# Copying attention values by DMA instead of ScalarE, stacking query and key parts with fewer transfers, and a new order table

## The reference

```
xn = layernorm(x)
s  = attention0(xn)      # 16 heads of 8, full 512x512 softmax      -> streams "A" and "head"
g  = silu(ffn0(xn))      # one of 8 experts per token               -> done for all rows before the loop
x  = x + s * g
xn = layernorm(x)
s  = attention1(xn)      # 16 local-window heads + 8 latent heads   -> stream "B"
g  = silu(ffn1(xn))      # two layers, each as below                -> stream "F" (and "finish")
x  = x + s * g

ffn1, per layer: h = shift_token(x); q, k, v = split(h @ wqkv)      # 8 heads of 64
                 q, k = rotary(l2norm(q) * qs), rotary(l2norm(k) * ks)
                 o = softmax(8 * q k^T, window of 64 and the one before) v ;  x = x + o @ wo
                 h = layernorm(shift_token(x)) ; x = x + (a * gelu(g)) @ w2, with a, g = split(h @ w1 + b1)
```

## Time and profile before

| | |
|---|---|
| median of 3 executions | 4537.1 us (4527.5 to 4545.72) |
| the profiled execution | 4527.5 us, its span 4525.7 us |
| busy PE | 3647.1 us (81%) |
| busy DVE | 2793.2 us (62%) |
| busy ACT | 2096.0 us (46%) |
| busy POOL | 734.8 us (16%) |
| DMA | 141.05 MB, 8.8% of 16 engines for the hardware queue |
| mean granted TensorE clock | 0.895 |
| the 13 full iterations | 813.3 to 4074.4 us of the span: 250.9 us each |

### The profile page before, as it was taken

How to read it: one execution, slowest core, us unless ns; L and a number is a source line. 1 busy time by engine, 2 the same in 40 slices (tenths; PEclk the granted TensorE clock), 3 DMA queues, 4 the chain that set the end, 5 groups by cost and what they waited for, 6 DMA issues and landing times. The chain is left out here.

```text
span 4525.7 us, 98207 instructions
## 1 busy us (share of the span) xinstructions
PE 3647.1 (81%) x41689; PEld 2067.7 (46%) x41816; DVE 2793.2 (62%) x5577; ACT 2096.0 (46%) x3692; POOL 734.8 (16%) x383
## 2 busy tenths in 40 slices
PE   3486788888878788888888788888888787888866
PEld 3372335444454545354444545353444445453543
DVE  5114467666666767666666666676666666676644
ACT  1122345555545454545545454545555454545533
POOL 3410011111111111111111111111111111111111
PEclk9996689898999999898989999898999998998978
DMA  4351101010000101010100101010100001010000
GB/s 144 117 170 45 26 21 26 23 26 19 20 18 23 25 21 27 24 26 24 26 19 11 27 22 26 21 26 24 26 19 26 13 23 25 21 27 23 4 10 3
DMA packets 130874, 141.05 MB, mean 31 GB/s; under 512 B 18005, under 2 KB 112703, under 8 KB 129855
## 3 DMA queue, kind: packets, MB, share of 16 engines
q1 hardware_dynamic: 120656, 105.16, 8.8%
q0 software_dynamic: 9712, 28.85, 2.1%
HBM read 81.27 MB, written 35.39 MB: 26 GB/s over the span
## 5 line engine op out<-in xcount | busy, mean ns | idle before, releaser
L964 ACT ACTIVATE prob_a<-bank 128x512 f32<-128x512 f32 x1024 | 585.5, 599 | 541.8 <-PE bank L909 538.3
L1016 DVE TENSOR_REDUCE nmax_a<-bank 128x1 f32<-128x512 f32 x768 | 513.1, 688 | 393.9 <-PE bank L882 388.4
L1358 POOL TENSOR_TENSOR rn<-ss,minus_half 128x16 f32<-128x16 f32 x128 | 489.8, 3827 | 1264.5 <-DVE ss L1632 1264.5
L1517 ACT ACTIVATE area<-bank 128x512 f32<-128x512 f32 x640 | 349.5, 601 | 291.0 <-PE bank L1409 223.5
L909 PE MATMUL bank<-Qst_a,Kst_a 74*128 74x512 bf16 x1024 | 411.5, 422 | 68.8 <-DVE nmax_a L1016 62.9
L896 PE MATMUL bank<-prob_a,V_a 128*9 128x512 f32 x2048 | 320.5, 703 | 51.1 <-ACT prob_a L964 48.3
L882 PE MATMUL bank<-Kst_a,Qst_a 72*128 72x512 bf16 x768 | 330.9, 431 | 31.3 <-ACT prob_a L964 15.9
L1635 DVE TENSOR_TENSOR prob_f<-area,rotf 128x1024 f32<-128x1024 f32 x256 | 308.0, 1225 | 1.0
L1409 PE MATMUL bank<-wqkv_s,hT 128*128 128x512 f32 x384 | 215.5, 685 | 82.9 <-issue 71.7
L1005 DVE TENSOR_REDUCE nmax_a<-bank 128x1 f32<-128x512 f32 x256 | 169.5, 687 | 109.7 <-PE bank L870 107.0
L909 PEld LDWEIGHTS bank<-Qst_a,Kst_a 74*128 74x128 bf16 x1024 | 98.2, 100 | 297.3 <-DVE nmax_a L1016 190.7
(11 more groups left out here) (282 smaller groups left out, 7153.0 us busy)
## 6 DMA issues: line engine op xcount, KB each, us to landing
Qst_a<-dq_a SPq DMA_DIRECT2D x192, 96.0 KB
Kst_a<-dk_a SPq DMA_DIRECT2D x192, 96.0 KB
dq_a<-prob_a SPq DMA_DIRECT2D x80, 128.0 KB, 2.4
dk_a<-prob_a SPq DMA_DIRECT2D x48, 128.0 KB, 2.4
area<-xs_d SPq DMA_DIRECT2D x39, 128.0 KB, 4.5
ys_d<-otok_f SPq DMA_DIRECT2D x39, 128.0 KB, 1.8
xs_d<-prob_f SPq DMA_DIRECT2D x4, 1024.0 KB, 8.9
x_a<-in_x_in SPq DMA_DIRECT2D x16, 256.0 KB, 2.9
```

The source lines that it names most:

```text
L964: nc.scalar.activation(dst, bk.full(act, product)[0:rows, :], func, **kw).then_inc(a_emptied["act"], 1)
L1016: nc.vector.tensor_reduce(out=nmax_a[:, g, t, j:j + 1], in_=bk.full(dve, f)[:], op=ALU.max, axis=AX.X, negate=True).then_inc(emptied, 1)
L1358: nc.gpsimd.tensor_tensor(rn[:, t % 2], ss[:, t % 2], minus_half[:], ALU.pow).then_inc(f_root, 1)
L1517: ins = nc.scalar.activation(dst, fk.full(act, product)[rows, cols], func, **kw)
```

## The change

Three edits and a new table.

**Values.** ACT writes only `V_f`. At the slot `QKV + 13` of each layer SP waits until the last V_f tile is brought, and copies `V_f` into `V_s` with two transfers: 64 partitions x 2080 floats, and 64 partitions x 1560 floats. PE waits for both (`f_moved`) before the first `values_f` of a layer. The initial memset of V_s's ones column goes, since the copies carry the column.

**Stacks.** `spill` still issues 8 transfers, but writes three full rotations of the q parts and three copies of the k parts (6 x 384 KB in place of 8 x 128 KB). `load_stack` then needs 2 transfers of 72 partitions for a group in place of 6 of 24 partitions. An inner row in DRAM is up to 3 KB, not 1 KB.

**Tables.** A_TIMES, H_TIMES and the three tables of F_AT for PE, ACT and DVE hold other numbers.

```diff
-A_TIMES = ((14, 15, 106, 113), (0.5, 2.7, 101.3, 102.4))
+A_TIMES = ((14, 15, 106, 113), (3.2, 3.7, 102.3, 103.4))
...
-        dq_a, dk_a = scratch("dq_a", [H0, 2 * SPLIT - 1, D0, T]), scratch("dk_a", [H0, SPLIT, D0, T])
+        dq_a, dk_a = scratch("dq_a", [H0, SPLIT, D0, SPLIT, T]), scratch("dk_a", [H0, SPLIT, D0, SPLIT, T])
...
-            for c in range(2 * SPLIT - 1):
-                sp.dma_start(dq[:, c], parts_q[:, c % SPLIT, :]).then_inc(s, 16)
-                if c < SPLIT:
-                    sp.dma_start(dk[:, c], parts_k[:, c, :]).then_inc(s, 16)
+            for i in range(SPLIT):
+                sp.dma_start(dq[:, i, :, 0:SPLIT - i, :], parts_q[:, i:SPLIT, :]).then_inc(s, 16)
+                if i:
+                    sp.dma_start(dq[:, i, :, SPLIT - i:SPLIT, :], parts_q[:, 0:i, :]).then_inc(s, 16)
+                sp.dma_start(dk[:, i], parts_k).then_inc(s, 16)
...
-            for i in range(SPLIT):
-                sp.dma_start(Qst[rows * i:rows * i + rows], q_rows[D0 * i:D0 * i + rows]).then_inc(s, 16)
-                sp.dma_start(Kst[rows * i:rows * i + rows], k_rows).then_inc(s, 16)
+            for stack, d in ((Qst, dq), (Kst, dk)):
+                sp.dma_start(stack[0:STACK], d[h:h + n].rearrange("h i d c t -> (i d c) h t")).then_inc(s, 16)
...
+            for l in range(DEPTH):
+                yield LAYER_AT + LAYER * l + QKV + 13
+                sp.wait_ge(*fk.brought(("fv", l, NT - 1), "act"))
+                sp.dma_start(V_s[0:FW], V_f[0:FW]).then_inc(f_moved, 16)
+                sp.dma_start(V_s[FW:P, 1:NT], V_f[FW:P, 0:NT - 1]).then_inc(f_moved, 16)
...
+                    if c == 0:
+                        pe.wait_ge(f_moved, 32 * (l + 1))
...
-                        nc.scalar.activation(V_s[0:FW, t, :, 0:FD], v[0:FW], ACT.Copy)
-                        yield at + 0.9
-                        if t + 1 < NT:
-                            nc.scalar.activation(V_s[FW:P, t + 1, :, 0:FD], v[FW:P], ACT.Copy)
-                            yield at + 1
```

More of the change, by code:

```diff
@@ L58 @@
 A_GROUP = (15, 37, 60, 84)
-A_TIMES = ((14, 15, 106, 113), (0.5, 2.7, 101.3, 102.4))
+A_TIMES = ((14, 15, 106, 113), (3.2, 3.7, 102.3, 103.4))
 B_TIMES = ((0, 1, 4, 5, 17, 25), (121.6, 126, 135.3, 142, 166, 185))
-H_TIMES = ((0, 30), (122.1, 194.3))
+H_TIMES = ((0, 30), (122.1, 195.9))
 FEED = ((0, 180), (0, 296))
 F_AT = {"sync": FEED, "gpsimd": FEED,
-        "tensor": ((1, 4.3, 4.6, 6.42, 8.55, 10.2, 11, 11.5, 11.8, 12.1, 13, 20.1, 21, 27.2, 29, 35.2, 37, 40, 42,
[7 rows of a table removed]
-        "scalar": ((1, 6.17, 8.55, 11.2, 12.3, 12.4, 20.4, 27, 27.2, 40, 42.6, 47, 60.8, 65.2, 68.5, 88.5, 90.2, 90.6,
[4 rows of a table removed]
-        "vector": ((4, 6.55, 7.1, 8.8, 12.5, 14, 22, 25.2, 26, 28.5, 29, 30, 34, 38.2, 39, 77, 79, 83, 87, 95, 101,
[4 rows of a table removed]
+        "tensor": ((1, 4.6, 6.05, 8.05, 8.55, 11.2, 11.5, 13, 19.8, 20.1, 21, 37, 46.4, 48.4, 50.8, 52, 53.1, 53.4,
[6 rows of a table added]
+        "scalar": ((1, 6.17, 8.55, 11.2, 12.3, 20.1, 20.3, 27.2, 40, 42.6, 52, 56.4, 65.2, 68.5, 78, 90.4, 90.6, 93.2,
[3 rows of a table added]
+        "vector": ((4, 6, 6.55, 7.1, 8.3, 8.8, 13.4, 13.6, 20, 20.5, 22, 28.5, 30, 33, 38.2, 39, 52.8, 53.1, 57.5, 79,
[6 rows of a table added]
 B_AT = 5
@@ L680, in _ @@
                         outputs_out(j - 2)
-                for V in (V_f, V_s):
-                    nc.vector.memset(V[:, :, :, FD:FD + 1], 1.0)
+                nc.vector.memset(V_f[:, :, :, FD:FD + 1], 1.0)
         def engine_sems(p):
@@ L705, in mixer_kernel @@
         a_var, a_rstd, b_var, b_rstd = sem("a_var"), sem("a_rstd"), sem("b_var"), sem("b_rstd")
-        f_sq, f_root, f_rot, f_mparts = (sem(n) for n in ("f_sq", "f_root", "f_rot", "f_mparts"))
+        f_moved, f_sq, f_root, f_rot, f_mparts = (sem(n) for n in ("f_moved", "f_sq", "f_root", "f_rot", "f_mparts"))
         f_wo, f_mid = sem("f_wo"), sem("f_mid")
@@ L796, in spill @@
         def spill(sp, parts_q, parts_k, dq, dk, s):
-            for c in range(2 * SPLIT - 1):
-                sp.dma_start(dq[:, c], parts_q[:, c % SPLIT, :]).then_inc(s, 16)
-                if c < SPLIT:
-                    sp.dma_start(dk[:, c], parts_k[:, c, :]).then_inc(s, 16)
-        SPILLED, STACKED = (3 * SPLIT - 1) * 16, 2 * SPLIT * 16
-        def load_stack(sp, dq, dk, h, n, Qst, Kst, s):
-            rows = SPLIT * D0
-            q_rows, k_rows = (d[h:h + n].rearrange("h c d t -> (c d) h t") for d in (dq, dk))
-            for i in range(SPLIT):
-                sp.dma_start(Qst[rows * i:rows * i + rows], q_rows[D0 * i:D0 * i + rows]).then_inc(s, 16)
-                sp.dma_start(Kst[rows * i:rows * i + rows], k_rows).then_inc(s, 16)
+            for i in range(SPLIT):
[3 more added lines that the diff above has]
+                sp.dma_start(dk[:, i], parts_k).then_inc(s, 16)
+        SPILLED, STACKED = 8 * 16, 2 * 16
+        def load_stack(sp, dq, dk, h, n, Qst, Kst, s):
+            for stack, d in ((Qst, dq), (Kst, dk)):
+                sp.dma_start(stack[0:STACK], d[h:h + n].rearrange("h i d c t -> (i d c) h t")).then_inc(s, 16)
         def max_to_stack(sp, mT, Qst, landed):
@@ L1560, in f_scalar @@
                         ps = fk.full(act, ("fv", l, t))
-                        v = ps[:].rearrange("p (h d) -> p h d", d=FD)
-                        nc.scalar.activation(V_s[0:FW, t, :, 0:FD], v[0:FW], ACT.Copy)
-                        yield at + 0.9
-                        if t + 1 < NT:
-                            nc.scalar.activation(V_s[FW:P, t + 1, :, 0:FD], v[FW:P], ACT.Copy)
-                            yield at + 1
-                        nc.scalar.activation(V_f[:, t, :, 0:FD], v, ACT.Copy).then_inc(f_emptied["act"], 1)
+                        nc.scalar.activation(V_f[:, t, :, 0:FD], ps[:].rearrange("p (h d) -> p h d", d=FD), ACT.Copy)\
+                            .then_inc(f_emptied["act"], 1)
                 yield s0 + 39
```

## The result

The changed kernel takes 4593.05 us (median of 4, 4576.43 to 4601.14) against 4541.16 before: the ratio is 1.0114, 95% interval 1.0079 to 1.0151. It is 52 us slower, where 43 us less were forecast. The profiled execution has a span of 4581.8 us, 56.1 more than before. Of these, 38.9 lie in the 13 full iterations, the next group. The others lie ahead of them and needn't be the change's. At the first iteration with F the changed kernel is 14.2 us late (591.5, not 577.3), but so are two kernels of the experiments whose code is the old one up to there, by 10.6 and 14.5 us. In the stretch before it the granted clock was 0.64 in the one profiled execution of the kernel before, and 0.57 and 0.56 in theirs. In the next group the columns are those of the earlier trace rows; the second and third stretch are the start of one full iteration and its stretch from 187.8 to 196.1 us.

What follows compares the result with a forecast made beforehand. PE was the busiest engine, 2747.6 of 3261.1 us, but engines wait for each other at an iteration's start. 4537.1 - 43 (ACT relief) + 2 (stacks) = 4496, stated as 4494 us; copies and order nothing; range 4428 to 4562.

Steps and rivals of the forecast that it cites:

- part two: Value copies by DMA, V_f to V_s: 6 us each, 9 at the end, hidden before V_s's first use, so costing nothing.
- the cover: Time from the last V_f copy to the first use of V_s, 26.8 us where shortest, said to hide the copies.
- The doubling by the rule on 64 partitions: Transfers confined to 64 partitions reach half the ports, so value copies take about double, some 12 us, still within 26.8.
- Part one: Value copies leave ACT, shortening PE's waits for hT_f, `area` and at L860: 2.7 us per iteration, 43 us over 16 rows.
- The wait for `area`: PE's wait for ACT at the scores L1385: 0.7 us less per iteration, between 0 and 1.9.
- The wait for gate_b: PE's wait for ACT at L860: 0.5 us less per iteration, between 0 and 0.8.
- Part three: Bigger spill, fewer stack loads: hidden in iterations with F, +1 us in each of two exposed ones, range -2 to +26.
- Part four: New order mid-iteration: attention0's projection up to 2.8 us later, F's x_f product sooner by about the same; taken as 0.
- The slower rival: Mid-iteration, projection and B start 2.8 us later in 15 iterations: about 4575 us; chance 0.18, shared with unhidden copies.
- copies that don't stay hidden: Value copies over 27 us, or SP's wait delaying the fourth stack: 4540 to 4580 us; within the slower 0.18.

## Why the prediction was wrong

| kernel | ratio | stop, 13 iterations |
|---|---|---|
| tables | 0.9966 | 21.6 |
| tables, late second load | 0.9929 | 18.3 |
| values by DMA | 1.0033 | 54.5 |
| new stacks | 1.0051 | 43.1 |
| tables, values by DMA in layer one | 0.9918 | 18.1 |
| the same and late second load | 0.9916 | 18.1 |
| tables, values by DMA in both | 1.0101 | 87.5 |
| the same, layer two's copies in seven | 1.0010 | 41.1 |
| tables, values by DMA in both, new stacks (the change) | 1.0114 | 81.8 |
| the change, layer two's copies late | 0.9985 | 39.4 |
| the change, layer two's values by ACT | 0.9983 | 39.0 |
| before, layer two's copies by DMA too | 1.0061 | 50.3 |
| before, same bytes to DRAM | 0.9994 | 32.2 |

**The step that failed is part two.** It put the copies by DMA at nothing: "So it costs nothing, even at three times the end." In the changed kernel PE's stop grew from 32.1 to 81.8 us over the 13 iterations, 3.8 us each, and each way of taking layer two's copies out of that place or cutting them up gave 40 to 56 us back. I counted the cover only for the one who reads V_s, and it held: PE never waits for V_s at L1450, and nothing in the loop waits for a stack. The DMA engines have another user that I didn't count, the instruction packets. Two signs of it were in the trace of before: a wait of PE "for issue" of 32.1 us in L1164, and a row of the page:

```profile
q8 instruction: 355, 5.82, 0.5%
```

I hadn't asked what ended that wait. The price was mis-sized too: 6 us, at most 9, where layer two's copies, queued behind stack loads, took 11.3 and 13.3. Behind no loads, layer one's took 4.7 and 6.0 in the same iteration; the page's medians over both layers (count, KB, us to landing) hide the difference:

```profile
V_s<-V_f SPq DMA_DIRECT2D x32, 520.0 KB, 4.7
V_s<-V_f SPq DMA_DIRECT2D x32, 390.0 KB, 6.0
```

The doubling by the rule on 64 partitions that the prediction cites can't be read from these: 12 us would fit layer two's, and 6 layer one's.

**Why so much more with the new tables.** The copies alone cost 0.33%, on top of the tables 1.35% (0.9966 to 1.0101). With the old tables, in 6 of the 13 iterations an instruction packet starts up to 0.2 us ahead of the copies' first packet (at 186.5 to 187.6 us), and PE hardly stops (0.7 to 1.6 us); in the others it stops for 5.0 to 7.6. With the new ones the copies are issued some 2.5 us earlier (median 183.6, not 186.1), no instruction packet is ahead of them, and all 13 iterations stop for 4.8 us or more (3.8 in the changed kernel). The time at which PE goes on follows the instruction packet, so what tables and ACT had gained before that point is waited out there: the changed kernel comes 1.9 us earlier to the group and leaves it 2.5 us later. This may also be why the terms don't add up. That reading rests on the iterations' own times in the traces; no run moved the issue alone by 2 us.

**Part one was right for hT_f and wrong for `area`.** I had 1.5 us per row for hT_f, and the wait fell by (36.0 - 15.0) / 13 = 1.6. It falls only in kernels whose first layer's copies are by DMA: with the copies alone it is 16.7, with the tables alone 37.0, and with layer one's copies added to the tables 15.0. By the ratios that step is worth 0.48% (0.9966 to 0.9918), some 22 us, where 16 x 1.5 = 24 stood in the sum; by the medians it is 15. The wait for `area` fell by 1.7 us per iteration, not 0.7, but the copies have no part in it. First the kernel with the copies alone, then the one with the tables alone, against 24.4 before:

```profile
PE bank L1389 <- ACT area L1523: 24.4, 39, 0.9
```

```profile
PE bank L1385 <- ACT area L1517: 2.5, 13, 0.2
```

The wait for gate_b (0.8 us) goes with either edit alone. Against them stands a new one, 16.7 at L1411 for hT_f, 1.3 per iteration, which the tables bring. At the stop the mean lead was 1.9 us, where 2.7 were summed. That tables and layer one's copies together gain 0.82%, some 37 us and near the 41 of the sum, is partly luck: 0.34% of it is the tables', which I had at nothing.

**Part three was right on the new tables, from a row read wrongly.** The 35.6 us of the earlier trace rows aren't two waits of 17.8. They are one wait, in the iteration with the head alone, counted once for PE and once for its weight loads:

```profile
PEld bank L870 <- DMA Kst_a<-dk_a: 18.0, 1, 18.0
PE bank L870 <- DMA Kst_a<-dk_a: 17.7, 1, 17.7
```

In the iteration of row 0 PE waits about 1 us for a stack in both kernels. The spill takes 10 us from first issue to first load (3790.83 to 3800.75), not 6.9, and that lies open once, with 3.1 us, where +2 in all stood in the sum:

```profile
PE bank L867 <- DMA Kst_a<-dk_a: 20.8, 1, 20.8
```

Beside the same kernel without the new stacks the change is 0.13% slower, less than the intervals. Alone, on the old tables, they cost 0.51%, of which the traces place 11 us in the stop and 3 in the head's iteration; the other 10 stay open.

**Part four and its rival.** I had taken 0 for the order, with a slower case in which the projection and B come late. The tables alone are 0.34% faster. B isn't late: its transposes start 147.5 us into the iteration, before 147.2, and its scores are earlier. The slower rival had the right sign and was 18 us off (about 4575, and 4593 came), for a reason that didn't hold, so that was luck; its second form, copies that don't stay hidden, asked only for a wait at L1446 or L882, and neither came.

## What to carry to other kernels

Before transfers are put on a queue as "hidden", look for every user of the DMA engines in that stretch, instructions among them: a wait of an engine "for issue" in the middle of a group whose inputs are there, with a packet of the instruction queue at its end, points to an engine that is out of instructions. Long transfers should then stay out of stretches with many small instructions (here groups of 128 matmuls and weight loads, and a 16 KB packet every 4 to 6 us), be cut into short packets (one run here, which also spread the issues), or be held back by a wait on the issuing engine. And a part that is slower in sum can hold a gain: undone in the right half (layer two's copies back on ACT, stacks as before), the change became 0.8% faster than before.

## What the runs showed of the hardware

- Instructions come by the same DMA engines as the data, in packets of 16 KB on queue 8. That TensorE waits for them is inferred from the times: the longest stop in one group ended 2.2 to 3.9 us after the start of a 16 KB instruction packet in all 13 iterations of 14 kernels.
- Equal bytes aren't equal cost: 8320-byte packets took 0.66 us each from SBUF to 64 partitions of SBUF, and 0.32 us to DRAM. With the first the stop grew by 18 us and the kernel became 0.6% slower, part of it away from the stop; with the second neither changed.
- The same bytes to the same partitions in packets of 2080 bytes, in seven transfers and not two, gave back 40 us.
- After a stop of 8.2 us TensorE's granted clock was 0.59 over the next 10 us, after one of 3.1 us 0.66.
